# First layer's experts of a Flamingo-like network: GpSimd waits for counts of TensorE between groups of four row scatters

## Chip, cores and metric

One core of a Trainium2 chip runs the whole program. The metric is the device time of one execution in microseconds (us).

## What is computed

The program is a stack of four layers. Each has an attention over a context, followed by a feed-forward block. It works on 16 sequences of 128 tokens with 256 features, 2048 tokens in all. The change lies in the first layer's feed-forward block, a mixture of experts:

```python
xf = x.reshape(-1, c)                              # 2048 tokens x 256, normalised
probs = softmax(xf @ gate_w.T)                     # 8 experts
top_p, top_i = top_k(probs, 2)                     # 2 experts for each token
...
h = silu(xf @ expert_fc1[e].T) * (xf @ expert_fc2[e].T)   # 176 wide, for each expert e
out_e = h @ expert_proj[e].T
y = sum over the two chosen experts of top_p * out_e
...
shared = (silu(xf @ shared_fc1.T) * (xf @ shared_fc2.T)) @ shared_proj.T    # 704 wide, for all tokens
y = y + sigmoid(xf @ shared_gate_w.T) * shared
```

## The kernel before

Each engine gets its program as a plain list of instructions, and semaphores tie the engines together. A `Mark` is such a semaphore: `then_inc(*mark.up())` counts it up by one, and `wait_ge(*mark.at(n))` waits until it has been counted up n times in this stage.

**The shared expert** runs in column steps. The 2048 tokens are 4 blocks of 512 and the 704 columns are 6 chunks of 128 (the last of 64), so there are NV = 24 steps v. Step v has an up part on TensorE (`pe_up`, L1043, matmuls at L1052), which counts `upped`. Then come a tanh on ScalarE (`act_tanh`, L1238, L1243), which waits for `upped.at(v + 1)` and for `silued.at(v - 2)`, two products on VectorE (`dve_gate`, L1181, L1187 and L1189), which count `silued` and `gated`, and a down part on TensorE (`pe_down`, L1055, L1064), which waits for `gated.at(v + 1)`. TensorE's order (`pe_program`, L1068) is up(v), down(v - 1). Up(v) waits for `gated` of two steps before, because it uses one of two PSUM places. Steps 0 to 17 run before the experts (LATE = 18), and the last six run after them.

**The routing** is spread over the same steps. After step 9 VectorE has the two slots of each token (`dve_tiles`, `dve_slots`, L1175). Each counts `slots_ready`.

**The scatters.** GpSimd then writes each token's row of 258 numbers to two slots in HBM (`pool_scatter`, L1264): 16 sequences for the first list of slots, k = 0, and 16 for the second, 32 indirect DMAs of 128 rows each, counted in `scattered`. It does so in `pool_program` (L1268):

```python
for k in range(2):
    pool.wait_ge(*slots_ready.at(k + 1))
    for b in range(NB):
        pool_scatter(b, k)
```

**The experts** (`experts`, L1296) take the slots in 39 tiles of 128 rows. For each tile, GpSimd gathers its expert's weights from HBM with an indirect DMA (`pool_gather`, L1485, 128 rows of 4864 bytes) into one of 8 places. The first 8 gathers stand right behind the scatters on GpSimd. Gathers 6 and 7 wait for `upped.at(LATE)`, since their places hold the shared expert's input until then, and gather n from 8 on waits for tile n - 8 to be done. GpSimd also stores each tile's result (`pool_store`, L1491). SyncE waits for all 32 scatters and then loads the slots' rows, two tiles at a time (`sp_load_rows`, L1523). TensorE turns a tile's rows (L1317), multiplies them up (L1329, which waits for the rows and the weights), turns the hidden part (L1337) and multiplies down (L1348). It begins with this when its shared steps up to 17 are done.

Of the kernel before, what the change touches and what calls it, by code (L numbers as in the profile page):

```python
# [920 lines left out]
def l0_ffn(m, ahead, wide, l1):  # L921

    nc, A = m.nc, m.A
    pe, dve, act, pool, sp = nc.tensor, nc.vector, nc.scalar, nc.gpsimd, nc.sync
# [51 lines left out]
    upped, projected, x_shared = m.mark("f_upped"), m.mark("f_downed"), m.mark("x_shared")  # L976
# [5 lines left out]
    LATE = NV - NF0  # L982
# [277 lines left out]
    def pool_roots(blk):  # L1260
        for n in range(blk * BLK, blk * BLK + BLK):
            ln_root(m, n, var_ready, rstd_ready)

    def pool_scatter(b, k):  # L1264
        pool.indirect_dma_start(out=x_slots[:, :], out_offset=bass.IndirectOffsetOnAxis(ap=slot_t[k][:, b:b + 1], axis=0),
                                in_=rows_t[:, b, k], in_offset=None, bounds_check=NROW0 * P - 1, oob_is_err=False).then_inc(*scattered[k].up(16))

    def pool_program():  # L1268
        for blk in range(1, NBLK):
            pool_roots(blk)  # L1270
        pool.wait_ge(*cleared.at(1 + 16 * N_CLEAR0))
        pool.wait_ge(*set_ready.at(4))
        pool.wait_ge(*rows_copied.at(NBLK))
        for k in range(2):
            pool.wait_ge(*slots_ready.at(k + 1))
            for b in range(NB):
                pool_scatter(b, k)


# [272 lines left out]
    def program():  # L1552
        sp_program()
        dve_program()
        pe_program()
        act_program()
        pool_program()
        experts()
# [2958 lines left out]
```

## Time and profile before

| | |
|---|---|
| median of 3 runs | 2018.48 us |
| lowest, highest | 2017.74, 2019.39 us |
| span of the profiled execution, first to last instruction | 2027.5 us |
| the profiled execution's own time, with what lies around the span | not given |
| TensorE matmul busy | 1723.9 us, 85% of the span |
| VectorE, ScalarE, GpSimd busy | 1370.3, 943.0, 787.8 us |
| mean granted TensorE clock | 0.949 |
| moved by DMA | 200.35 MB in 180430 packets, mean 99 GB/s |

The profile is that of one execution, recorded by the hardware. The runs that give the median are executions without recording. A busy engine is one that executes; waiting, branching and issuing instructions on the sequencers are not busy time, except that on GpSimd an indirect DMA shows for the time in which its descriptors are made, about 1 us, and not for that in which its data moves. In the rows "<-" in brackets names what ended an engine's idle time: another engine's instruction, "issue" (no wait ended just then by what the profile shows) or "remote" (a semaphore was counted up, and the profile doesn't tell by whom).

### The profile page before, as it was taken

How to read it: one execution, taken by the hardware profiler on the slowest of the kernel's cores; microseconds unless marked ns; L12 is line 12 of the kernel's file. 1: busy time of each engine (PE TensorE's matmuls, PEld its weight loads, DVE VectorE, ACT ScalarE, POOL GpSimd, SP SyncE). 2: the span in 40 equal slices, each digit the busy share in tenths (PEclk: the TensorE clock that was granted, in tenths of full speed). 3: DMA queues.
4: the chain of work that ended last, by engine and by line, in shares of the span. 5: the costliest groups of instructions: out<-in, count | busy, mean ns of one | idle time of the engine just before them, and what ended most of it. 6: DMA issues, size and time to landing. Idle time of an engine off the chain costs nothing.

```text
span 2027.5 us, 35050 instructions
## 1 busy us (share of the span) xinstructions
PE 1723.9 (85%) x12191; PEld 1177.6 (58%) x12221; DVE 1370.3 (68%) x3299; ACT 943.0 (47%) x2227; POOL 787.8 (39%) x957
## 2 busy tenths in 40 slices
PE   6888889949897888888796877788999999887898
PEld 2444434626665777777684555455766766665445
DVE  7888874514367888888747888854666667566446
ACT  2666663203323677676644565324444444433352
POOL 3333321245655555554525553220133333333340
PEclk7999999979998999999898999899999999999898
DMA  4444422037953333433113542036010000030767
GB/s 106 104 123 93 98 46 91 29 144 259 296 142 87 76 83 80 90 80 69 62 43 101 163 111 79 5 119 225 1 35 19 30 10 1 13 94 2 237 210 298
DMA packets 180430, 200.35 MB, mean 99 GB/s; under 512 B 86500, under 2 KB 150129, under 8 KB 176928
## 3 DMA queue, kind: packets, MB, share of 16 engines
q1 hardware_dynamic: 161920, 155.92, 28.3%
q0 software_dynamic: 15168, 41.54, 6.0%
q8 instruction: 99, 1.62, 0.3%
q10 hardware_dynamic: 3168, 0.66, 0.2%
q14 instruction: 75, 0.61, 0.1%
HBM read 131.88 MB, written 75.44 MB: 102 GB/s over the span
## 4 chain that ended last, share of the span: by engine, by line
PE 46%; DVE 23%; issue 11%; ACT 10%; POOL 4%; DMA 3%; ACTq 1%; SPq 1%; another core or an unknown queue 0%; DVEq 0%; POOLq 0%
PE psum L3390 3%; PE psum L389 3%; PE psum L3464 3%; PE psum L3457 3%; ACT sbuf L3826 2%; PE psum L1052 2%; DVE sbuf L539 2%; PE psum L1329 2%; PE psum L352 2%; PE psum L3439 2%; PE psum L2276 2%; PE psum L1348 2%; PE psum L3426 2%; PE psum L1064 1%; ACTq L674 1%
## 5 line engine op out<-in xcount | busy, mean ns | idle before, releaser
L3826 ACT ACTIVATE sbuf<-psum,sbuf 128x128 f32<-128x128 f32 x256 | 113.7, 454 | 177.1 <-DVE sbuf L3638 162.7
L539 DVE TENSOR_REDUCE sbuf<-psum 128x2 f32<-128x512 f32 x256 | 164.9, 686 | 36.0 <-PE psum L352 34.9
L190 POOL TENSOR_TENSOR sbuf<-sbuf 128x1 f32<-128x1 f32 x128 | 73.2, 574 | 293.5 <-DVE sbuf L182 293.2
L2011 ACT ACTIVATE sbuf<-psum 128x512 f32<-128x512 f32 x256 | 138.7, 594 | 72.4 <-PE psum L1764 67.4
L681 ACT ACTIVATE sbuf<-psum 128x1024 f32<-128x1024 f32 x128 | 130.4, 1021 | 37.1 <-PE psum L374 29.5
L3916 POOL DMA_INDIRECT l_slot_inputs<-sbuf x96 | 95.3, 992 | 100.6 <-DVE sbuf L3709 75.6
L3464 PE MATMUL psum<-sbuf 128*128 128x256 f32 x512 | 124.2, 386 | 4.9 <-DVE sbuf L3656 4.9
L3390 PE MATMUL psum<-sbuf 128*128 128x256 f32 x512 | 117.0, 382 | 0.8 <-ACT sbuf L3790 0.8
L352 PE MATMUL psum<-sbuf 112*128 112x256 bf16 x512 | 104.4, 288 | 14.1 <-DVE sbuf L539 7.4
L3390 PEld LDWEIGHTS psum<-sbuf 128*128 128x128 f32 x512 | 97.1, 192 | 20.6 <-issue 8.6
L3464 PEld LDWEIGHTS psum<-sbuf 128*128 128x128 f32 x512 | 93.8, 193 | 16.1 <-issue 5.8
L3457 PE MATMUL psum<-sbuf 128*128 128x512 f32 x128 | 70.4, 632 | 38.4 <-ACT sbuf L3834 33.4
L352 PEld LDWEIGHTS psum<-sbuf 112*128 112x128 bf16 x512 | 41.7, 102 | 92.7 <-DVE sbuf L539 52.8
L1895 DVE TENSOR_REDUCE sbuf<-psum 128x8 f32<-128x1024 f32 x64 | 77.5, 1211 | 26.6 <-PE psum L1755 26.6
L3596 DVE COPY sbuf<-psum 128x1024 f32<-128x1024 f32 x32 | 39.2, 1224 | 72.7 <-ACT sbuf L3797 57.1
L1052 PE MATMUL psum<-sbuf 128*128 128x512 f32 (+1 forms) x192 | 87.6, 600 | 0.0
L2003 ACT ACTIVATE sbuf<-sbuf 128x128 f32<-128x128 f32 x256 | 81.4, 398 | 0.0
L1888 DVE TENSOR_REDUCE sbuf<-sbuf 128x8 f32<-128x1024 f32 x64 | 78.1, 1220 | 2.2
L1789 PE MATMUL psum<-sbuf 128*16 128x128 f32 x2048 | 71.6, 283 | 8.2 <-DVE sbuf L1902 6.8
L1886 DVE TENSOR_TENSOR sbuf<-psum,sbuf 128x1024 f32<-128x1024 f32 x64 | 77.6, 1212 | 1.1 <-PE psum L1743 1.1
L1764 PE MATMUL psum<-sbuf 128*128 128x128 f32 x512 | 71.8, 285 | 7.4 <-ACT sbuf L2011 7.3
L3439 PEld LDWEIGHTS psum<-sbuf 128*128 128x128 f32 x512 | 66.4, 196 | 14.9 <-issue 14.9
(436 smaller groups left out, 4478.9 us busy)
## 6 DMA issues: line engine op xcount, KB each, us to landing
l_pair_outputs<-sbuf SPq DMA_DIRECT2D x24, 512.0 KB, 6.7
sbuf<-in_l_gu_pairs SPq DMA_DIRECT2D x32, 384.0 KB, 8.5
sbuf<-l_pair_outputs SPq DMA_DIRECT2D x16, 768.0 KB, 15.9
sbuf<-l_q_parts SPq DMA_DIRECT2D x16, 384.0 KB
l_q_parts<-sbuf SPq DMA_DIRECT2D x64, 96.0 KB, 2.2
sbuf<-l_q_parts SPq DMA_DIRECT2D x32, 192.0 KB
l_k_parts<-sbuf SPq DMA_DIRECT2D x64, 96.0 KB, 2.2
sbuf<-l_k_parts SPq DMA_DIRECT2D x32, 192.0 KB
```

The source lines that it names most:

```text
L352: last = pe.matmul(score_bank[v % 2][:, j * T0:(j + 1) * T0], q3[0:STACK + 48, h, c * P:(c + 1) * P], k3[0:STACK + 48, h // 4, :], start=T ...
L539: dve.tensor_reduce(top3[:, 2 * hp:2 * hp + 2, c], score_bank[v % 2].rearrange("p (j t) -> p j t", j=2), AXX, ALU.max, negate=True).then_i ...
L681: act.activation(e_t[u % 12], shift_bank[u % 2], ACT.Exp).then_inc(*exped.up())
L1052: last = pe.matmul(up_bank[v % 2][0:M, n * BANK:(n + 1) * BANK], wn[:, k, fs], xt_t[blk][:, k, :], start=(k == 0), stop=(k == KD - 1))
L2003: last = act.activation(d, d, ACT.Identity, bias=max_t[n % 3][:, j:j + 1])
L2011: act.activation(e_t[i % 4][:, h * BANK:(h + 1) * BANK], turn_bank[:, h * BANK:(h + 1) * BANK], ACT.Exp).then_inc(*exped.up())
L3390: last = pe.matmul(q_bank[:, j * N:(j + 1) * N], w.wq[:, k, (4 * g + j) * P:(4 * g + j + 1) * P], xt_t[pair % 2][:, k, :], start=(k == 0), ...
L3439: last = pe.matmul(score_bank[:, j * P:(j + 1) * P], q[:, 4 * g + j, i * P:(i + 1) * P], kT_t[b % 3][:, g * P:(g + 1) * P], start=True, st ...
L3457: pe.matmul(av_bank, v_t[b % 3][:, g * P:(g + 1) * P], eT_t[u % 2], start=True, stop=True).then_inc(*valued.up())
L3464: last = pe.matmul(out_bank[:, 0:D], o_t[b % 2][:, h * P:(h + 1) * P], w.wo[:, h, :], start=(h == 0), stop=(h == H3 - 1))
L3826: last = act.activation(e_t[u % 3][:, j * P:(j + 1) * P], score_bank[:, j * P:(j + 1) * P], ACT.Exp, bias=mt[:, j:j + 1], scale=rq[:, lo + ...
L3916: pool.indirect_dma_start(out=route.x_slots[:, :], out_offset=bass.IndirectOffsetOnAxis(ap=route.slot[b][:, k:k + 1], axis=0), in_=xr_t[b ...
```

## The change

GpSimd waits between groups of four scatters. The wait is for `upped`, TensorE's count of the shared expert's up steps. With LATE = 18 the groups (k, b) = (0, 4), (0, 8), (0, 12), (1, 0), (1, 4), (1, 8), (1, 12) wait for counts 12, 13, 14, 15, 16, 17, 18. The first group, (0, 0), waits for nothing new. No instruction is added otherwise, and none changes its place on its engine.

```diff
         for k in range(2):
             pool.wait_ge(*slots_ready.at(k + 1))
             for b in range(NB):
+                if b % 4 == 0 and (k or b):
+                    pool.wait_ge(*upped.at(LATE - 7 + 4 * k + b // 4))
                 pool_scatter(b, k)
```

## Rows read from the trace of the kernel before

**Rows 1.** The page: span, and busy time of each engine.
```profile
span 2027.5 us, 35050 instructions
PE 1723.9 (85%) x12191; PEld 1177.6 (58%) x12221; DVE 1370.3 (68%) x3299; ACT 943.0 (47%) x2227; POOL 787.8 (39%) x957
```

**Rows 2.** Waits, 380 to 470 us: waiting, releaser, us in total, times, longest.
```profile
ACT sbuf L1243 <- remote: 33.4, 2, 31.7
...
PE psum L1064 <- DVE sbuf L1189: 27.1, 2, 26.9
```

**Rows 3.** Windows: busy time of each engine, granted clock, DMA share, GB/s.
```profile
core 0: us, PE busy (x) PEld busy (x) DVE busy (x) ACT busy (x) POOL busy (x), PEclk, DMA share, GB/s
...
420.00:425.00 5.00, 0.00 (x0) 0.00 (x0) 0.00 (x0) 0.00 (x0) 3.78 (x5) 0.50 0.30 105
445.00:450.00 5.00, 5.00 (x12) 2.86 (x12) 0.54 (x1) 0.00 (x0) 0.00 (x0) 0.79 0.04 14
...
460.85:572.00 111.15, 101.33 (x465) 71.16 (x466) 44.96 (x198) 40.72 (x116) 72.80 (x72) 1.00 0.78 256
```

**Rows 4.** Timeline of TensorE: start, us, what, idle before.
```profile
396.33 3.60 PE L1052 MATMUL psum<-sbuf 128*128 128x512 f32 x8
...
401.78 3.70 PE L1052 MATMUL psum<-sbuf 128*128 128x512 f32 x8
...
407.04 3.60 PE L1052 MATMUL psum<-sbuf 128*128 128x512 f32 x8
...
412.84 3.60 PE L1052 MATMUL psum<-sbuf 128*128 128x512 f32 x8
...
459.94 0.66 PE L1317 MATMUL psum<-sbuf 128*128 128x128 f32 x4
460.85 1.45 PE L1329 MATMUL psum<-sbuf 128*128 128x352 f32 x4 [0.26 <-ACT sbuf L1441]
```

**Rows 5.** Timeline of ScalarE.
```profile
394.61 0.59 ACT L1243 ACTIVATE sbuf<-psum 64x512 f32<-64x512 f32 x1 [4.71 <-PE psum L1052]
399.96 0.60 ACT L1243 ACTIVATE sbuf<-psum 128x512 f32<-128x512 f32 x1 [4.77 <-issue]
408.91 0.60 ACT L1243 ACTIVATE sbuf<-psum 128x512 f32<-128x512 f32 x1 [8.35 <-issue]
441.22 0.60 ACT L1243 ACTIVATE sbuf<-psum 128x512 f32<-128x512 f32 x1 [31.71 <-remote]
443.50 0.60 ACT L1243 ACTIVATE sbuf<-psum 128x512 f32<-128x512 f32 x1 [1.68 <-remote]
450.63 0.60 ACT L1243 ACTIVATE sbuf<-psum 128x512 f32<-128x512 f32 x1 [6.54 <-PE psum L1052]
455.94 0.59 ACT L1243 ACTIVATE sbuf<-psum 64x512 f32<-64x512 f32 x1 [4.71 <-PE psum L1052]
```

**Rows 6.** Timeline of GpSimd: scatters (L1265), then gathers (L1485).
```profile
389.65 1.21 POOL L1265 DMA_INDIRECT l_slot_inputs<-sbuf  x1 [34.82 <-DVE sbuf L1175]
...
395.00 0.97 POOL L1265 DMA_INDIRECT l_slot_inputs<-sbuf  x1 [0.31 <-issue]
...
429.49 0.97 POOL L1265 DMA_INDIRECT l_slot_inputs<-sbuf  x1 [0.30 <-issue]
430.77 1.01 POOL L1485 DMA_INDIRECT sbuf<-in_l_expert_rows,sbuf  x1 [0.31 <-issue]
432.08 0.97 POOL L1485 DMA_INDIRECT sbuf<-in_l_expert_rows,sbuf  x1 [0.30 <-issue]
...
437.09 0.94 POOL L1485 DMA_INDIRECT sbuf<-in_l_expert_rows,sbuf  x1 [0.30 <-issue]
456.18 0.94 POOL L1485 DMA_INDIRECT sbuf<-in_l_expert_rows,sbuf  x1 [18.15 <-PE psum L1052]
...
556.35 0.96 POOL L1485 DMA_INDIRECT sbuf<-in_l_expert_rows,sbuf  x1 [1.54 <-DVE sbuf L1386]
```

**Rows 7.** Timeline of SyncE's queue: the first loads of slot rows.
```profile
432.05 1.42 SPq L1523 DMA_DIRECT2D sbuf<-l_slot_inputs  x3
```

## The prediction

> **What bounds the kernel now.** I read the page first, for the size of things. The profiled execution spans 2027.5 us, and TensorE is busy for 85% of it [rows 1]. That is no licence to cost the change by TensorE's share. The change touches one place, so the question is what ends last there.
>
> I then asked for the waits around that place, 380 to 470 us [rows 2]. Two entries stand out. ScalarE waited once for 31.7 us before a tanh of the shared expert (L1243), put down to "remote", which means that the view found a semaphore update but nobody who made it. TensorE waited 26.9 us for VectorE (L1189) before a down step (L1064). VectorE had nothing to do in that time because ScalarE's tanh had not come. The reader should see one pause here, told three times.
>
> The windows of that stretch [rows 3] show the pause from the side. From 420 to 425 us TensorE, VectorE and ScalarE do nothing at all. GpSimd is the only busy engine, and the DMA engines are at 0.30, so nobody is short of bandwidth. TensorE's granted clock is 0.50 there, its lower level (1.2 of 2.4 GHz), after an idle stretch. From 445 to 450 us it is 0.79, and later 1.00.
>
> The timeline says who waits for what. TensorE's up steps run 396.33 to 399.93, 401.78 to 405.48, 407.04 to 410.64 and 412.84 to 416.44 us [rows 4]. ScalarE's tanh follows the first of these at 399.96, after 0.03 us. It follows the second at 408.91, 3.4 us late. It follows the third at 441.22, 30.6 us late, and the fourth at 443.50, 27.1 us late. The next one is ordinary again [rows 5]. The tanh waits only for TensorE's count (`upped`) and for VectorE's step of three columns earlier, long done. So TensorE had executed its matmuls, and its count reached ScalarE 30 us later.
>
> GpSimd meanwhile issues without a break [rows 6]: 32 scatters from 389.65 to 430.46 us, then six weight gathers until 438.03. There it stops for 18.15 us, because gather 6 waits for `upped`. The late counts arrive 3.2 us after it stopped. In the burst, two counts came in time (394.6 and 400.0), and the first late one fell 16 us in.
>
> **Who sets the start of the experts.** In the profile TensorE does: its last shared step ends and the first expert tile follows at 459.94 us [rows 4], long after the rows were asked for at 432.05 [rows 7]. From there on GpSimd and the DMA engines set the pace. GpSimd issues a gather and a store for each tile, 39 gathers until 556.35 [rows 6], and the DMA engines are at 0.78 over the whole stage [rows 3]. Whatever moves the start of this stage moves its end by about as much.
>
> **Is the pause there in the timed runs?** The sum stands or falls with this. The span, which leaves out whatever lies before the first instruction and after the last, is 2027.5 us. The median of the runs without a profile is 2018.48, and the highest is 2019.39. The profiled execution is thus at least 9.0 us longer than the timed ones. (Its own time beyond the span is not given.) Something in it does not happen, or happens less, when nobody records, and the one stretch that looks like no ordinary wait is this pause. I take it to be mostly absent from the timed runs.
>
> The Trainium skill ("NOTIFIC — the notification-queue block", section 7.1) says that the block which collects trace records never drops one inside its own pipeline but pushes back, and that this can throttle an engine. By that rule the pause would belong to the recording alone and the change would gain nothing in the timed runs. The trace agrees in kind: the counts arrive in a heap after GpSimd stops. No row shows the block itself.
>
> **The change, part by part.** Seven waits are added on GpSimd, before scatters 4, 8, 12 of the first slot list and 0, 4, 8, 12 of the second. They wait for `upped` at 12, 13, 14 and 15, 16, 17, 18. No instruction is removed or moved. Behind a waiting scatter on GpSimd stand the other scatters, then the gathers. SyncE waits for all 32 scatters before it loads rows, and TensorE waits for rows and weights.
>
> Take a program without the pause. The ends of the four up steps are counts 13 to 16, so a step takes (416.44 - 399.93) / 3 = 5.50 us [rows 4]. Counts 17 and 18 would come at 421.9 and 427.4. Four scatters take (429.49 - 395.00) / 27 x 4 = 5.1 us [rows 6]. The group is a little shorter than the step, so GpSimd waits slightly more each time and ends up tied to TensorE. The last group starts at 427.4 + 0.26 us (GpSimd left its wait at 456.18 us [rows 6], when the count that ScalarE saw at 455.94 [rows 5] had come). It lasts 5.1 us, and the first gather starts at 432.8 us where it now starts at 430.77: **+2.0 us**.
>
> Is that on the path? TensorE would finish the shared steps about 4 us after count 18 (459.94 against 455.94 [rows 4, 5]), at 431.5 us. Rows are asked for at 432.05 [rows 7], and 1.6 us after the last scatter in both kernels, so TensorE waits for GpSimd and not the other way round. The 2.0 us goes through whole. Bounds: with the longest interval (5.8 us, 410.64 to 416.44) for both steps it is +2.6. With the shortest (5.16) it is +1.4. Zero is the floor if rows or weights land no later, because the DMA engines had slack. A gain is excluded in this case, since nothing is taken away. I take 2.0: 2018.5 + 2.0 = **2020.5 us**. The waits themselves cost nothing beyond this, as GpSimd is idle 0.30 us between scatters anyway [rows 6].
>
> In the profiled execution the same edit should do more. Bursts become at most four scatters long whenever a count is late, so the pause should shrink.
>
> **The rivals.**
>
> *The pause is real, and the waits remove it (faster).* For: the delay is in the trace, it ends 3.2 us after GpSimd falls silent, and the change makes GpSimd fall silent. Against: 9.0 us that the timed runs don't have. At best the first up step of the experts starts not at 460.85 [rows 4] but when gathers 0 and 1 have landed. That is no earlier than 434.7 (gather 1 is issued by 433.05 [rows 6], and the last scatter took 1.6 us to land, 430.46 to 432.05 [rows 7]) and no later than 446 us (the DMA engines are at 0.04 after 445 [rows 3]), each plus 2.0: a gain of 13 to 24 us. At worst every group of 5.1 us is followed by the 3.2 us that the counts needed after GpSimd's stop. Then groups 3 to 7 start 8.3 us apart from 408.5, count 18 comes by 441.7 instead of 455.9, and the first gather goes at 446.8. Gathers 0 and 1 take 3.9 to 15.2 us to be there (434.7 and 446 less 430.77), so the first expert step starts between 450.7 and 462.0. That leaves between nothing and 10 us of gain. Over both ends the gain is 0 to 24 us, the middle about 12.5: 2006.
>
> *The pause is real and has nothing to do with the bursts (slower).* GpSimd now inherits it. The group that waits for count 15 starts at 441.5 [rows 5] instead of about 410 (389.65 + 16 x 1.28). The next two follow at 446.6 and 451.7, their counts being there (443.50 and 450.63 [rows 5]). The last starts at 456.8, so the first gather goes at 461.9 instead of 430.77. Gathers 0 and 1 lay ready before and would now take 3.9 to 15.2 us. The first expert step then starts at 465.8 to 477.1 instead of 460.85, later by 5 to 16 us. I take +10 us, the middle: 2028.5. It decides as soon as a count comes more than some 2 us after TensorE's last matmul of its step and GpSimd's stop doesn't bring it on.
>
> *The change does nothing.* If the counts are there whenever GpSimd comes, the time stays. By the sum the margins are tenths of a us per group. This is the zero end of my own case.
>
> **How the numbers follow.** A difference under 0.2% (4 us) can't be told from no change here. My case (pause absent from the timed runs) gets 0.57. Of that, 0.51 stays within 0.2%, 0.05 is slower by more because a wait costs more than bounded, and 0.01 is faster by more. That the waits are all met in advance is part of it. The gain gets 0.30, of which 0.03 is too small to tell. The inherited pause gets 0.13, all of it slower. Faster 0.28, same 0.54, slower 0.18. The range reaches down to 2006, the middle of the gain's own range, which leaves out 0.15. It reaches up to 2029 to hold the price of the inherited pause, which leaves out some 0.05. My case's own range is 2018.5 to 2021.1, and the likeliest time in it is 2020.5.
>
> **What the profile of the changed kernel would show.** If I am right, the seven gaps on GpSimd are there, each under 1 us where TensorE is in step. ScalarE's tanh follows each up step within a us or a few, the 31.7 us wait is gone, and TensorE's clock stays at its upper level. The span falls by 10 us or more while the timed median does not fall. If the median falls with the span, the pause was real and my central step is wrong. If the long wait stands and GpSimd's first gather starts past 455 us, the third case holds. If GpSimd leaves its waits with lateness of 2 to 4 us each, the step that failed is my 5.5 us per step.

## The result, and the profile after

The changed kernel took 2011.84 us in the median of 7 runs (2002.85 to 2015.63). Beside it the kernel before took 2019.62 us in 7 runs (2017.74 to 2027.34). The ratio is 0.9933, with a 95% interval of 0.9911 to 0.9956: **faster by 0.7%**. (The ratio is the time of the edited kernel over that of the kernel before, here and below.) The forecast was no change (2020.5 us), and the gain was the first rival. The time lies in the range of 2006 to 2029, but it moved in a way that the forecast did not have. A few executions of any kernel here take far longer than all others (one of flush4_third 3467.8 us), and no ratio counts them.

The page of the changed kernel answers [rows 1] with a span 25.2 us shorter:

```profile
span 2002.3 us, 35081 instructions
```

The waits of the same stretch, 380 to 470 us, answer [rows 2]:

```profile
PE psum L1319 <- DMA sbuf<-l_slot_inputs: 9.7, 1, 9.7
...
ACT sbuf L1243 <- remote: 7.2, 1, 7.2
```

The wait of 31.7 us is gone, and with it TensorE's wait of 26.9 us. In their place TensorE waits 9.7 us for rows (L1317 of before is L1319 here). GpSimd's timeline answers [rows 6]:

```profile
389.39 1.21 POOL L1265 DMA_INDIRECT l_slot_inputs<-sbuf  x1 [33.19 <-DVE sbuf L1175]
...
395.10 0.97 POOL L1265 DMA_INDIRECT l_slot_inputs<-sbuf  x1 [0.64 <-issue]
...
400.76 0.97 POOL L1265 DMA_INDIRECT l_slot_inputs<-sbuf  x1 [0.86 <-issue]
...
424.32 0.97 POOL L1265 DMA_INDIRECT l_slot_inputs<-sbuf  x1 [2.96 <-remote]
...
434.56 1.01 POOL L1487 DMA_INDIRECT sbuf<-in_l_expert_rows,sbuf  x1 [0.30 <-issue]
...
540.46 0.96 POOL L1487 DMA_INDIRECT sbuf<-in_l_expert_rows,sbuf  x1 [1.38 <-PE psum L1350]
```

The gaps before the groups are 0.64, 0.86, 0.43, 0.40 and 0.52 us, then one of 2.96, and none before the last group. ScalarE's tanh, against [rows 5]:

```profile
405.26 0.60 ACT L1243 ACTIVATE sbuf<-psum 128x512 f32<-128x512 f32 x1 [4.95 <-PE psum L1052]
410.42 0.60 ACT L1243 ACTIVATE sbuf<-psum 128x512 f32<-128x512 f32 x1 [4.56 <-issue]
415.81 0.60 ACT L1243 ACTIVATE sbuf<-psum 128x512 f32<-128x512 f32 x1 [4.79 <-PE psum L1052]
423.58 0.60 ACT L1243 ACTIVATE sbuf<-psum 128x512 f32<-128x512 f32 x1 [7.18 <-remote]
426.04 0.59 ACT L1243 ACTIVATE sbuf<-psum 64x512 f32<-64x512 f32 x1 [1.86 <-PE psum L1052]
```

One count is still late. TensorE's up step ended at 420.71 and the tanh came at 423.58, 2.9 us later and 2.2 us after GpSimd had stopped at 421.36. TensorE and its clock, against [rows 4] and [rows 3]:

```profile
417.11 3.60 PE L1052 MATMUL psum<-sbuf 128*128 128x512 f32 x8
...
439.84 1.11 PE L1319 MATMUL psum<-sbuf 128*128 128x128 f32 x4 [9.72 <-DMA sbuf<-l_slot_inputs]
443.28 2.69 PE L1331 MATMUL psum<-sbuf 128*128 128x352 f32 x4 [2.33 <-issue]
```
```profile
420.00:425.00 5.00, 5.00 (x17) 2.41 (x16) 0.76 (x2) 0.60 (x1) 1.74 (x3) 1.00 0.15 53
...
435.00:440.00 5.00, 0.16 (x1) 0.17 (x2) 0.18 (x3) 0.00 (x0) 3.78 (x5) 0.50 0.74 244
```

The clock stays at its upper level through the shared steps and falls to the lower one only while TensorE waits for rows. TensorE pays for that at the start of the experts, where the first up step takes 2.69 us instead of 1.45. This step starts at 443.28 us instead of 460.85, 17.6 us earlier, and the last gather at 540.46 instead of 556.35, 15.9 us earlier. So the pause was worth some 16 us of this trace's 25.2. The other 9 lie behind the experts, where the change touches nothing (from the start of their last down matmul to the end it takes 1456.0 us before and 1447.0 after). Runs of one kernel differ by as much (2017.74 to 2027.34), and the two traces stand at opposite ends: this one took 2003.6 us against a median of 2011.84, and the one of the kernel before is longer than all seven timed runs.

### The profile page after: what moved, and what is told of

Read it like the earlier page. It is cut to its first block, busy times and chain, and to the rows that moved or that the text cites. A ratio compares the mean times of both kernels' runs of the same rounds, so it can differ in the third digit from the quotient of the medians.

```text
span 2002.3 us, 35081 instructions
## 1 busy us (share of the span) xinstructions
PE 1724.0 (86%) x12221; PEld 1177.1 (59%) x12221; DVE 1371.8 (69%) x3299; ACT 942.7 (47%) x2227; POOL 789.3 (39%) x957
## 4 chain that ended last, share of the span: by engine, by line
PE 46%; DVE 23%; issue 10%; ACT 10%; POOL 5%; DMA 4%; ACTq 1%; SPq 1%; another core or an unknown queue 0%; DVEq 0%; POOLq 0%
PE psum L3392 4%; PE psum L389 3%; PE psum L3466 3%; ACT sbuf L3828 3%; PE psum L3459 3%; PE psum L1331 2%; PE psum L1052 2%; DVE sbuf L539 2%; PE psum L352 2%; PE psum L3441 2%; PE psum L2278 2%; PE psum L3428 2%; PE psum L1350 2%; ACTq L674 1%; POOL l_slot_inputs L1265 1%
## 5 line engine op out<-in xcount | busy, mean ns | idle before, releaser
L681 ACT ACTIVATE sbuf<-psum 128x1024 f32<-128x1024 f32 x128 | 130.5, 1021 | 37.7 <-PE psum L374 28.2
L3392 PEld LDWEIGHTS psum<-sbuf 128*128 128x128 f32 x512 | 97.1, 192 | 20.7 <-issue 8.6
L3466 PEld LDWEIGHTS psum<-sbuf 128*128 128x128 f32 x512 | 93.2, 192 | 16.0 <-issue 5.8
L374 PE MATMUL psum<-sbuf 128*128 128x512 bf16 x256 | 77.9, 386 | 0.5 <-ACT sbuf L681 0.2
## 6 DMA issues: line engine op xcount, KB each, us to landing
sbuf<-l_pair_outputs SPq DMA_DIRECT2D x16, 768.0 KB, 15.6
```

What stands on the lines that cost most here:

```text
L681: act.activation(e_t[u % 12], shift_bank[u % 2], ACT.Exp).then_inc(*exped.up())
L3392: last = pe.matmul(q_bank[:, j * N:(j + 1) * N], w.wq[:, k, (4 * g + j) * P:(4 * g + j + 1) * P], xt_t[pair % 2][:, k, :], start=(k == 0), ...
L3466: last = pe.matmul(out_bank[:, 0:D], o_t[b % 2][:, h * P:(h + 1) * P], w.wo[:, h, :], start=(h == 0), stop=(h == H3 - 1))
```

## The experiments

The result named the pause as real but not its cause. It also left open whether the arithmetic of the forecast (+2.0 us without a pause) was right. Two theories of why the counts come late:

- **Run-ahead.** GpSimd's sequencer hands scatters to its engine faster than the engine works, and a full queue holds the counts up.
- **Silence.** The counts are held up while the engine makes descriptors for long without a stop.

The runs fell on different chips, and that turned out to matter more than any edit. The kernel before ran beside each of them on the same chip, and every ratio is taken on one chip. A count is called late when ScalarE's tanh starts over 1 us after TensorE's last matmul of the step.

| chip | kernel before, median | counts late in the traces | runs |
|---|---|---|---|
| 1 | 1986.92, 1987.51 us | no | after_again, lag8, flush4, early_waits, before_again, after_third |
| 7 | 1985.9 us | no | flush4_second, groups8, early_waits_second |
| 14 | 1989.9 us | can't be seen: all_late issues no scatter during these steps | all_late |
| 0 | 2018.52 us | yes | after_fourth, flush4_third |
| 6 | 2026.95 us | yes | lag8_second, before_second |
| 4 | 2030.31 us | yes, in two of three | flush4_fourth, early_waits_third, groups8_second |

The list of waits separates the chips as well. "remote" stands in it in each trace of an ordinary execution on chips 0, 4 and 6, and in none on chips 1, 7 and 14.

### The changed kernel again (after_again), no other edit

> The changed kernel once more, beside the others. Two theories of why TensorE's counts come late in the kernel before. Run-ahead: GpSimd's sequencer hands scatters to its engine faster than the engine works (one in 0.52 us against 1.28) until about twelve lie queued, and from then on counts of TensorE come late. Silence: what counts is how long the engine makes descriptors without a pause. Both expect here what the changed kernel gave: ratio 0.989 to 0.997, no tanh L1243 more than 4 us late, first gather at about 434.5 us.

Measured on chip 1: 1988.31 us, ratio 1.0003 (0.9987 to 1.0018). No tanh was late. The expectation was wrong: there was nothing to gain on this chip.

### A limit on the run-ahead (lag8)

```diff
+                g = 4 * k + b // 4
+                if b % 4 == 0 and g >= 2:
+                    pool.wait_ge(*scattered[(g - 2) % 4].at(64 * ((g - 2) // 4 + 1)))
                 pool_scatter(b, k)
```

(`scattered` is four semaphores here instead of two.)

> Before scatter group g of four, GpSimd waits until group g - 2 has landed. The engine has no pause of more than about 0.5 us, but at most some 7 scatters lie queued. It waits for nothing of TensorE. Run-ahead: the long wait before tanh L1243 goes, first gather within 1 us of 430.8 us, time as the changed kernel or up to 4 us less: ratio 0.987 to 0.996. Silence: the wait of about 30 us stands, ratio 0.998 to 1.002.

Measured on chip 1: 1987.35 us, ratio 1.0003 (0.9985 to 1.0021). It tells nothing of the theories, since no count was late there.

### Stops without TensorE (flush4)

```diff
+                if b % 4 == 0 and (k or b):
+                    pool.memset(zeros, 0.0).then_inc(*gap.up())
+                    pool.wait_ge(*gap.now())
                 pool_scatter(b, k)
```

> Between groups of four scatters GpSimd clears a buffer of zeros once more (128x258) and waits for that, so that its queue runs dry seven times and its engine makes no descriptors for some 0.6 to 1 us each time. Nothing of TensorE is waited for. Run-ahead: no late counts, first gather at 435 to 438 us, ratio 0.990 to 0.998. Silence: a pause under 1 us in 6 helps little; some count is late by 3 us or more after 16 us of scatters, as in the changed kernel, and the ratio lies between 0.993 and 1.002.

Measured on chip 1: 1993.29 us, ratio 1.0038 (1.0022 to 1.0055). The first gather came 46.75 us behind the first scatter. That is 5.5 us more than in the kernel before (41.21, below), and the stops were a plain cost.

### Waits that are always met (early_waits)

```diff
+                if b % 4 == 0 and (k or b):
+                    pool.wait_ge(*upped.at(8))
                 pool_scatter(b, k)
```

> The same seven waits in the same places, each for the count 8, which TensorE has reached at 383 us, before the first scatter. They are always met. Both theories expect the kernel before: wait of about 30 us before tanh L1243, first gather at 430.8 us, ratio 0.998 to 1.002. If it is faster, the wait instructions themselves do it and not the pausing.

Measured on chip 1: 1988.25 us, ratio 1.0006 (0.9989 to 1.0022). No tanh was late here either, with GpSimd issuing without a break. Either the seven empty waits prevent it or the chip does, so I needed the trace of the kernel before on such a chip.

### The kernel before on chip 1 (before_again), and the changed one (after_third)

> The kernel before, unchanged, to have its trace beside the others' on their chip. So far two theories of the long wait are left. Chip: the wait of 31.7 us belongs to the chip (or to its recording) on which the first profile was taken, where releasers read remote; on the chip of the four runs since, the kernel before has no late count, every tanh L1243 follows its up step within 0.1 us, the first gather stands 41.1 us behind the first scatter as in early_waits, and the span is 1980 to 1992 us. Instructions: the seven waits as such prevent it on any chip, whether they are met or not; then this run shows a late tanh and a span above that of early_waits (1981.5 us) by 10 us or more.

> The changed kernel beside before_again on the same chip. Where no count is late: first gather 42.5 us behind the first scatter, 1.4 us more than in the kernel before, time within 0.3% of it. On a chip where counts are late: faster by 0.4 to 1.3%.

Measured: 1986.53 us, ratio 0.9998 (0.998 to 1.0016), and 1987.01 us, ratio 0.9991 (0.9974 to 1.0009). This is the same program as in [rows 5], on another chip. The timeline of ScalarE in before_again, and its wait for `upped` in the waits from 380 to 470 us:

```profile
405.82 0.60 ACT L1243 ACTIVATE sbuf<-psum 128x512 f32<-128x512 f32 x1 [4.95 <-PE psum L1052]
410.99 0.60 ACT L1243 ACTIVATE sbuf<-psum 128x512 f32<-128x512 f32 x1 [4.56 <-PE psum L1052]
416.14 0.60 ACT L1243 ACTIVATE sbuf<-psum 128x512 f32<-128x512 f32 x1 [4.56 <-PE psum L1052]
421.31 0.60 ACT L1243 ACTIVATE sbuf<-psum 128x512 f32<-128x512 f32 x1 [4.56 <-PE psum L1052]
```
```profile
ACT sbuf L1243 <- PE psum L1052: 42.6, 9, 5.2
```

There is no "remote" in the whole list of waits, all nine tanh waits are put down to TensorE's matmuls, and the longest is 5.2 us. So the program alone doesn't make the pause, and the empty waits didn't prevent it. What differs is the chip. GpSimd's timeline gives the arithmetic of the forecast a clean test: first scatter and first gather, in before_again and then in after_third.

```profile
389.96 1.21 POOL L1265 DMA_INDIRECT l_slot_inputs<-sbuf  x1 [34.82 <-DVE sbuf L1175]
...
431.17 1.01 POOL L1485 DMA_INDIRECT sbuf<-in_l_expert_rows,sbuf  x1 [0.30 <-issue]
```
```profile
389.06 1.21 POOL L1265 DMA_INDIRECT l_slot_inputs<-sbuf  x1 [33.19 <-DVE sbuf L1175]
...
431.57 1.01 POOL L1487 DMA_INDIRECT sbuf<-in_l_expert_rows,sbuf  x1 [0.30 <-issue]
```

That is 41.21 us before and 42.51 after: **+1.3 us**.

### What a late first gather costs (all_late)

```diff
+                if k == 0 and b == 0:
+                    pool.wait_ge(*upped.at(LATE))
                 pool_scatter(b, k)
```

> One wait in place of seven: all 32 scatters wait for count 18, the last up step before the experts. This prices a delay of the first gather. If a delay on GpSimd goes through to the end in full (the prediction's rule), the first scatter starts at about 427 us instead of 390, the first gather at 468 instead of 431, and the time grows by 35 to 39 us, ratio 1.0175 to 1.0195, where no count is late. If the stage absorbs part of it (weights gathered faster later on, tiles bound by TensorE), the ratio is under 1.015. On a chip where counts come late, the tanh steps are all in time, because TensorE's steps then run while GpSimd issues nothing, and the time lies near the kernel before, ratio 1.000 to 1.015.

Measured on chip 14, 2 runs: 2026.0 us, ratio 1.0175 (1.0121 to 1.0229). The first gather starts at 468.91 us, 37.7 us later than in before_again, and 0.0175 x 1989.9 = 34.8 us arrive at the end. With two runs the interval is wide (24 to 46 us). The full delay lies in it, and so does two thirds of it.

### lag8 and the kernel before where counts are late (lag8_second, before_second)

> lag8 again, in the hope of a chip on which counts come late (chips on which the kernel before takes about 2018 us or more, against about 1987). There, by the run-ahead theory, no tanh is over 4 us late and the ratio is 0.985 to 0.996, and by the silence theory the long wait stands and the ratio is 0.998 to 1.002. On a chip without late counts: ratio 0.998 to 1.002, first gather 41.2 us behind the first scatter.

> The kernel before, for its trace on the same chip. Where counts are late: long wait of 20 us or more before a tanh L1243, semaphore updates put down to remote, span above 2015 us. Elsewhere: no remote at all, span 1980 to 1992 us.

Measured on chip 6: lag8 2033.96 us, ratio 1.0031 (1.0003 to 1.0059), slightly slower than expected, and the kernel before 2028.0 us, ratio 0.9994 (0.9977 to 1.0011). The timelines of lag8_second (its line 1244 is L1243 of before, and 1266 is L1265), ScalarE first:

```profile
407.16 0.60 ACT L1244 ACTIVATE sbuf<-psum 128x512 f32<-128x512 f32 x1 [6.23 <-PE psum L1053]
440.97 0.60 ACT L1244 ACTIVATE sbuf<-psum 128x512 f32<-128x512 f32 x1 [33.21 <-remote]
443.93 0.60 ACT L1244 ACTIVATE sbuf<-psum 128x512 f32<-128x512 f32 x1 [2.36 <-remote]
```
```profile
401.76 0.97 POOL L1266 DMA_INDIRECT l_slot_inputs<-sbuf  x1 [0.31 <-DMA l_slot_inputs<-sbuf]
...
406.87 0.97 POOL L1266 DMA_INDIRECT l_slot_inputs<-sbuf  x1 [0.30 <-DMA l_slot_inputs<-sbuf]
```
```profile
L1266 POOLq MOVE  x32: 29/29/35, 389.1 to 424.0; - x32
```

The waits are there (released by landings), the engine still idles only 0.30 us between scatters, and the count comes as late as ever. The last row is the sequencer's part of the scatters. It reaches the last one at 424.0 us, 5.9 us before the engine (429.87). In the kernel before it was 15.6 us ahead (413.9 against 429.49), and in the changed kernel, which has only one count slightly late, 5.7 us (427.6 against 433.28). Equal run-ahead goes with a long pause in one kernel and with almost none in the other: **the run-ahead theory falls.**

before_second shows the pause in another shape: tanh waits of 23.3 and 12.8 us, put down to "remote".

```profile
431.92 0.60 ACT L1243 ACTIVATE sbuf<-psum 128x512 f32<-128x512 f32 x1 [23.31 <-remote]
```

TensorE had ended that step at 412.59, and GpSimd issued from 391.59 to 440.06 us with no gap above 0.31. So this count came 19.3 us late, but in the middle of the issuing and not after a stop.

### Three on chip 7 (flush4_second, groups8, early_waits_second)

groups8 has three of the seven waits:

```diff
+                if b % 8 == 0 and (k or b):
+                    pool.wait_ge(*upped.at(LATE - 7 + 4 * k + b // 4))
                 pool_scatter(b, k)
```

> flush4 once more, for a chip on which counts come late; lag8_second has felled the run-ahead theory there. Silence theory: what helps is that GpSimd's engine stops making descriptors, whatever it stops for. The stops of flush4 (about 1 us after every 5.1 us, 5.5 us in all) then work as those of the changed kernel: no tanh more than 5 us late, ratio 0.988 to 0.998 where the kernel before takes over 2015 us. If only a stop that lasts until TensorE's count has come helps (pacing theory), some tanh is over 8 us late and the ratio is over 0.998. On a chip without late counts: ratio 1.002 to 1.006 as in flush4.

> Three waits instead of seven: before scatters (0, 8), (1, 0), (1, 8), for counts 13, 15, 17. On a chip with late counts: bursts of 8 scatters last 10.2 us, and the first count after them has to come before the next burst starts, so no wait of 20 us or more; ratio 0.988 to 0.998. On a chip without: GpSimd waits hardly at all, ratio 0.998 to 1.002, first gather 41.2 to 42.0 us behind the first scatter.

> Seven waits that are always met. On a chip with late counts both theories expect the long wait (over 20 us, remote) as in the kernel before, ratio 0.998 to 1.002; without it, the wait instructions alone would be what helps. On a chip without late counts: ratio 0.998 to 1.002.

Measured, all without a late count: flush4 1.0045 (1.001 to 1.0081), groups8 1.0028 (1.0006 to 1.005), early_waits 1.0018 (0.9983 to 1.0053). groups8 is slower than the 0.998 to 1.002 that was expected. Its first gather stands 42.3 us behind the first scatter, 1.1 more than in the kernel before on chip 1.

### The changed kernel on chip 0 (after_fourth, flush4_third)

> The changed kernel. On a chip with late counts: ratio 0.989 to 0.997 and no wait of over 8 us before a tanh L1243. On a chip without: ratio 0.998 to 1.002, no remote.

> flush4 on the same chip as after_fourth. On a chip with late counts, by the silence theory no tanh is over 5 us late and the ratio is 0.988 to 0.998; by the pacing theory some tanh is over 8 us late and the ratio is over 0.998. On a chip without late counts: ratio 1.002 to 1.006.

Measured: the changed kernel 2006.92 us against 2018.52, ratio 0.9959 (0.993 to 0.9987). One tanh wait is of 7.2 us, "remote", as in the first trace of the changed kernel. flush4_third gave one time to compare, 2005.35 us, too few for a ratio, and no trace of it.

### Three on chip 4, with late counts (flush4_fourth, early_waits_third, groups8_second)

> On a chip with late counts, by the silence theory no tanh L1243 is over 5 us late and the ratio is 0.988 to 0.998 (the one undisturbed run of flush4_third was 2005.35 us against a median of 2018.52). By the pacing theory some tanh is over 8 us late and the ratio is over 0.998. On a chip without late counts: ratio 1.002 to 1.006.

> On a chip with late counts: the long wait (over 20 us before a tanh, remote) as in the kernel before, ratio 0.998 to 1.002. On a chip without: the same ratio and no remote.

> On a chip with late counts: no wait of 20 us or more before a tanh, since a late count now stops GpSimd within 8 scatters; ratio 0.988 to 0.998. On a chip without: ratio 0.999 to 1.004.

Measured against 2030.31 us: flush4 2018.4 us, ratio **0.9933** (0.9909 to 0.9958); early_waits 2030.99 us, ratio 1.0015 (0.9993 to 1.0036); groups8 2013.93 us, ratio 0.9945 (0.9905 to 0.9986). ScalarE in early_waits_third:

```profile
409.65 0.60 ACT L1243 ACTIVATE sbuf<-psum 128x512 f32<-128x512 f32 x1 [9.17 <-remote]
441.97 0.60 ACT L1243 ACTIVATE sbuf<-psum 128x512 f32<-128x512 f32 x1 [31.72 <-remote]
```

In flush4_fourth, ScalarE and then GpSimd around one stop:

```profile
410.07 0.60 ACT L1243 ACTIVATE sbuf<-psum 128x512 f32<-128x512 f32 x1 [4.56 <-PE psum L1052]
415.23 0.60 ACT L1243 ACTIVATE sbuf<-psum 128x512 f32<-128x512 f32 x1 [4.56 <-PE psum L1052]
420.39 0.60 ACT L1243 ACTIVATE sbuf<-psum 128x512 f32<-128x512 f32 x1 [4.56 <-PE psum L1052]
```
```profile
393.12 0.97 POOL L1267 DMA_INDIRECT l_slot_inputs<-sbuf  x1 [0.31 <-issue]
394.08 0.34 POOL L1280 MEMSET sbuf<- 128x258 f32 x1
395.20 0.97 POOL L1267 DMA_INDIRECT l_slot_inputs<-sbuf  x1 [0.78 <-issue]
```

On the same chip, one kernel has the long wait and the other has not one late tanh. The seven stops last 1.1 us between two scatters (0.34 of memset, 0.78 idle) and know nothing of TensorE. Empty waits do nothing. In groups8_second the bursts are twice as long. One tanh is 5.3 us late (TensorE's step ended at 413.63), and it comes while GpSimd is still in its burst, which lasts until 419.25. The next is 3.2 us late, and GpSimd's own wait grows to 3.45 us:

```profile
418.98 0.60 ACT L1243 ACTIVATE sbuf<-psum 128x512 f32<-128x512 f32 x1 [9.88 <-PE psum L1052]
```

So on such chips short stops of GpSimd keep the counts in time, whatever they wait for. (This rests on one trace and eight times of one chip.) That the change works in the same way is an inference: its own stops are shorter, all but one (0.40 to 0.86 us idle instead of 0.30). What stays open is whether it is the stops or the lower rate of scatters. Four took 5.1 us in the kernel before and in lag8, 5.2 to 5.7 in the changed kernel (one late count, in the 24th scatter) and 5.9 in flush4 (none). No run tells the two apart. Nor is silence needed for a late count to arrive: those at 408.91 in [rows 5], at 431.92 in before_second and at 418.98 in groups8_second came while GpSimd issued.

## Why the prediction was wrong

**The step that failed** is the one under "Is the pause there in the timed runs?": that the profiled execution is at least 9.0 us longer than the timed ones, so that "something in it does not happen, or happens less, when nobody records". The result lists for every run of the changed kernel its span and its granted clock, and each time is its span plus 1.3 or 1.4 us (2003.6 and 2002.3). So the timed runs were recorded too, unlike what the section on the time and profile before says, and profile and timed runs did not differ in that. Seven runs of the kernel before then spread from 2017.74 to 2027.34 us. The three of the forecast lay at the bottom of this spread, and the profiled execution just above its top (2027.5 + 1.3 = 2028.8 us). (The 9.0 us is also the distance to the median. To the highest of the three it was 8.1.) The distance was no evidence on the pause. Whether it is spread alone or also another chip is open, as no chip is given for this first pair. The pause was in the timed runs. With it in, the right case was the first rival, whose mechanism (stops of GpSimd keep the pause away) flush4_fourth shows at work. Its price was 0 to 24 us, the middle 12.5. The medians fell by 7.8 and, on chip 0, by 11.6 us, and the ratios give 13.5 and 8.3 us.

**The rule that I leaned on**, of the Trainium skill ("NOTIFIC — the notification-queue block", section 7.1), that a block collecting records can hold up an engine, was given weight because it fitted the step above. Whether recording causes the pause stays open. Every run here was recorded, on chips with the pause and on chips without it. The runs show only that the same program, recorded in the same way, has no pause on chip 1.

**What held, where no count is late.** The forecast of +2.0 us for a program without the pause was right in kind. Measured on chip 1, the first gather moves by +1.3 us and the time by a ratio of 1.0003 and 0.9991, no change. Two terms of the sum were off, in opposite directions. The first is the 5.50 us per step. From count 13 to 18 before_again takes (426.61 - 400.27) / 5 = 5.27 us a step. The longest of the three steps that I averaged over, the 5.80 us to 416.44, was itself lengthened by the pause that the sum leaves out: the tanh before it was 3.4 us late, and TensorE stood idle for its down part. The row of the kernel before, and the same one of before_again, where this step took 5.16 us:

```profile
411.01 1.99 PE L1064 MATMUL psum<-sbuf 128*128 128x256 f32 x8 [0.37 <-issue]
```
```profile
410.79 1.89 PE L1064 MATMUL psum<-sbuf 128*128 128x256 f32 x8
```

So count 18 comes 36.6 us behind the first scatter in after_third, and not 37.8. The second term is the 0.26 us from the count to the scatter, which took 0.8 (425.68 to 426.46). With 5.1 us for the last group, as forecast, that gives 42.5. "The 2.0 us goes through whole" agrees with what was measured, but a delay this small can't be seen in a time. In the traces the first expert up step of after_third comes 1.0 us later behind the first scatter than in before_again, for 1.3 on GpSimd. Larger delays: all_late 34.8 of 37.7 us, and flush4 5.5 us on GpSimd, 7.6 and 8.9 us in time.

**Other points.** TensorE does wait for GpSimd's rows once the pause is gone (9.7 us, and 5.78 in before_again). "The span falls by 10 us or more while the timed median does not fall": the span fell by 25.2 and the median fell with it, which was named as the sign that the central step is wrong. The seven gaps were under 1 us, but for one of 2.96. The second rival, an inherited pause, did not occur: GpSimd waited 2.96 us at most, and the last gather came 15.9 us earlier.

**Where the rest of a slow chip's time goes.** The difference between [rows 4] (460.85) and before_again (439.68) at the first expert up step is 21 us. Between first up and last down matmul of the experts lie 110.7 us on the first chip (460.8 to 571.5) and 99.1 us in before_again (439.7 to 538.8):

```profile
L1348 PE MATMUL psum<-sbuf x156: 377/379/483, 465.4 to 571.5; 88*128 88x256 f32 x156
```
```profile
L1348 PE MATMUL psum<-sbuf x156: 377/379/483, 446.4 to 538.8; 88*128 88x256 f32 x156
```

GpSimd issues almost without a break there too, and the waits of that stage on such chips name "remote" as well. Late counts may be what makes it longer. No run here shows it. The change leaves this part alone: 112.0 us in its first trace (443.3 to 555.3).

## What to carry to other kernels

A span beside three medians doesn't tell whether a stall in the trace is real. Look first how far runs of one kernel spread, and whether the timed runs were recorded as the profile was. When a semaphore's count arrives long after the instruction that makes it and the profile puts the wait down to "remote", take the trace of the same kernel on a second chip before pricing any edit. Here the edit was worth 0.4 to 0.7% on two measurements with late counts and nothing, or a few tenths of a per cent of cost for the like, where no count was late.

## What the hardware showed unexpectedly

- TensorE's counts can reach ScalarE and GpSimd 30 us late while GpSimd issues indirect DMAs back to back (38 in 48 us), with the DMA engines at 0.30 (420 to 425 us). Counts came late on three of the six numbered chips (0, 4, 6). On chips 1 and 7 none did, and chip 14 has no trace that could show it.
- A count is first late by over 1 us after 16 us of such issuing (21 us in before_second). Where the wait lasts until GpSimd stops, the count comes about 2 to 5 us after that, but some late counts come while it issues.
- A stop of 1.1 us after every four scatters kept all counts of these steps in time in flush4_fourth, and limiting the scatters that have not landed to eight did not in lag8_second.
- The kernel before takes 1986 to 1990 us in the median on chips 1, 7 and 14 and 2018 to 2030 us on chips 0, 4 and 6.
